# Earlier bias transfers, a new order of the first stage, and four products of batch 1 on GpSimd

## The reference

```python
x = x + L0(x)   # masked softmax over blocks of 128 tokens, pooled @ x, divided by the count
x = x + L1(x)   # zX*lap_x + zY*lap_y + zR*y*(1-y); lap_x along the 512 channels, lap_y along tokens
x = x + L2(x)   # z = relu(x@Wd + bd); y = x + z@Wu + bu; layernorm(y)*g + b
x = x + L3(x)   # below
# L3: ctx = causal_ema(x); wg = sigmoid([x, ctx] @ Wg + bg); h1 = gelu(x @ Wn1 + bn1)
#     mod = 0.5 + sigmoid(h1 @ Wn2 + bn2); traces_d = causal_ema(x*wg*mod_d)
#     gate = sigmoid(blend(traces) @ Wtemp + btemp); soma = gelu(x @ Wsoma + bsoma)
#     out = layernorm((soma*gate) @ Wout) * gamma + beta
```

## Time and profile before

| | us |
|---|---|
| median of 3 runs | 744.46 (743.62 to 744.91) |
| profiled execution | 746.6 |
| its span | 744.8 |
| PE busy | 676.6 (91%) |
| DVE busy | 539.8 (72%) |
| ACT busy | 351.0 (47%) |
| POOL busy | 175.4 (24%) |

### The profile page before, as it was taken

One profiled execution on the slowest core, in us unless ns is written; L12 is line 12 of the kernel. 1 busy time (PEld: TensorE's weight loads), 2 busy tenths in 40 slices (PEclk: granted clock), 3 DMA queues, 4 the chain that ended last, 5 costly groups with the idle time before them and its releaser, 6 DMA issues.

```text
span 744.8 us, 7950 instructions
## 1 busy us (share of the span) xinstructions
PE 676.6 (91%) x2808; PEld 495.2 (66%) x2808; DVE 539.8 (72%) x736; ACT 351.0 (47%) x710; POOL 175.4 (24%) x220
## 2 busy tenths in 40 slices
PE   4979976465699999999999999999999999999996
PEld 1544443234486877787777868786877787787874
DVE  3558984458799669667875976697669768875964
ACT  1142475254445733563465347344733563465144
POOL 5004337425344110220032111202210220031001
PEclk9989998867899999999999999999999999999999
DMA  7991698668944474147326434551474050314001
GB/s 211 296 389 65 179 298 200 130 191 288 295 107 79 57 147 80 57 76 150 58 70 131 82 57 113 116 95 20 110 153 74 0 114 2 56 19 96 0 2 56
DMA packets 52470, 87.87 MB, mean 118 GB/s; under 512 B 8256, under 2 KB 10304, under 8 KB 52430
## 3 DMA queue, kind: packets, MB, share of 16 engines
q0 software_dynamic: 16896, 33.56, 27.9%
q1 hardware_dynamic: 32046, 53.79, 21.0%
q10 hardware_dynamic: 3488, 0.01, 0.3%
HBM read 64.27 MB, written 23.09 MB: 117 GB/s over the span
## 4 chain that ended last, share of the span: by engine, by line
PE 77%; DVE 12%; DMA 3%; issue 3%; ACT 2%; POOL 1%; SPq 1%; POOLq 0%; DVEq 0%; ACTq 0%
PE bank L1051 20%; PE bank L1053 19%; PE bank L1052 19%; PE bank L1107 4%; PE bank L1091 3%; PE bank L1047 2%; PE bank L1154 2%; DMA xr<-rows_scratch 2%; PE bank L1116 2%; PE bank L952 2%; PE bank L1081 2%; DVE xts L1411 2%; DMA xts<-in_xT 1%; DVE xb L1398 1%; DVE xts L1404 1%
## 5 line engine op out<-in xcount | busy, mean ns | idle before, releaser
L1506 DVE TENSOR_TENSOR_SCAN tr<-alpha,carry,tr 128x512 f32<-128x512 f32 x48 | 58.9, 1268 | 0.0
L1500 DVE SCALAR_TENSOR_TENSOR tr<-wgb,blend_w,mod 128x512 f32<-128x512 f32 x64 | 46.0, 750 | 10.7 <-ACT mod L765 9.9
L546 POOL TENSOR_TENSOR xts<-xb 128x2040 f32<-128x2040 f32 x8 | 31.5, 3937 | 93.5 <-DVE xb L1398 59.1
L1051 PE MATMUL bank<-xh,wg_l 128*128 128x512 f32 x128 | 53.0, 414 | 0.0
L1051 PE MATMUL bank<-th,wg_l 128*128 128x512 f32 x128 | 52.0, 406 | 0.0
L1052 PE MATMUL bank<-xl,wg_h 128*128 128x512 f32 x128 | 50.6, 395 | 0.0
L1053 PE MATMUL bank<-xh,wg_h 128*128 128x512 f32 x128 | 50.4, 393 | 0.0
L1053 PE MATMUL bank<-th,wg_h 128*128 128x512 f32 x128 | 50.1, 391 | 0.0
L1052 PE MATMUL bank<-tl,wg_h 128*128 128x512 f32 x128 | 49.9, 390 | 0.0
L1398 DVE SCALAR_TENSOR_TENSOR xb<-bank,rnorm,xb 128x512 f32<-128x512 f32 x32 | 23.7, 748 | 31.5 <-PE bank L1048 31.5
L780 ACT ACTIVATE carry<-tr 128x2 f32<-128x2 f32 x32 | 6.5, 203 | 74.8 <-DVE tr L1506 74.8
(11 more groups left out here) (246 smaller groups left out, 1963.0 us busy)
## 6 DMA issues: line engine op xcount, KB each, us to landing
x2b<-beside_scratch POOLq DMA_DIRECT2D x12, 1024.0 KB, 10.3
xr<-rows_scratch POOLq DMA_DIRECT2D x10, 1024.0 KB, 9.6
xb<-in_x SPq DMA_DIRECT2D x8, 1024.0 KB, 14.6
beside_scratch<-xb SPq DMA_DIRECT2D x8, 1024.0 KB, 6.2
result<-xr SPq DMA_DIRECT2D x7, 1024.0 KB, 10.5
local_scratch<-xts SPq DMA_DIRECT2D x6, 1024.0 KB, 9.3
x2b<-local_scratch SPq DMA_DIRECT2D x6, 1024.0 KB, 5.5
x2b<-rows_scratch POOLq DMA_DIRECT2D x6, 1024.0 KB, 9.4
```

The source lines that it names most:

```text
L546: po.tensor_tensor(side[:, :, 1:E - 1], xg[:, :, 0:E - 2], xg[:, :, 2:E], ALU.add)\
L1051: pe.matmul(acc, wl, xh_, start=start, stop=False)
L1500: ve.scalar_tensor_tensor(t[:, d], w, blend_w[:, d, k:k + 1], mod[:, d], ALU.mult, ALU.mult).then_inc(tr_in, 1)
L1506: ve.tensor_tensor_scan(t[:, d], alpha[:, 1 + d:2 + d].broadcast_to([P, GN]), t[:, d], 0.0 if first else carry[:, k, 1 + d:2 + d], ALU.mul ...
```

## The change

Two kinds of edit. First, bias and order: the bias row of L2 is added to x2 as the first of its three adding transfers (for blocks 0 and 1 when their stencil is done, for the others when the block is back from DRAM, one or two turns ahead); so the transposed x2 holds the bias, and `x2_evict` takes it off again with `-up_cols`. `y_sum` has no wait for it any more. The orders of all five engines in stage 1 change, the parameter work of DVE moves to the front in smaller pieces, `load_adapter(1)` and others move in SP's list, the tiles xh, xl, x2b1, hb1 and wn2_rep are laid out otherwise, and the wait for `local_done` before the copies of wn2 is gone. Second, `by_local(4)` to `by_local(7)` go from DVE to POOL, each ahead of the `channels` of its block.

```diff
+x2b1 = sb2("x2b1", [P, GT, E])
+xh = sb2("xh", [P, KE, GN], F32R)
+xl = sb2("xl", [P, KE, GN], F32R)
-sb2("between", [P, 1280])
-xh = sb2("xh", [P, KE, GN], F32R)
-xl = sb2("xl", [P, KE, GN], F32R)
-x2b1 = sb2("x2b1", [P, GT, E])
...
-mix_v = sem("mix_v")
+mix_v = [sem(f"mix_v{b}") for b in range(B)]
...
     for i, t in enumerate((row_bu, row_s)):
         sp.dma_start(rows_dram[b:b + 1, i], t[2 * Q * b:2 * Q * b + 1]).then_inc(rows_out, 16)
 store_beside(0)
-store_beside(1)
 sp.wait_ge(rows_out, 16 * 2 * B)
 sp.dma_start(gamma_row[:], row(gamma, P)).then_inc(rows2_in, 16)
 for b in range(B):
     pid = sp.value_load(ids[0:1, b:b + 1], min_val=0, max_val=7)
     sp.dma_start(ln_g_row[:, b], ln_g[bass.ds(pid, 1), :].broadcast_to([P, E]))\
       .then_inc(rows2_in, 16)
+store_beside(1)
 sp.wait_ge(hid_mm, 2 * NG)
 sp.dma_start(wg_st[:, 0:KE], chunks(wg)[:, 0:KE]).then_inc(w_in[0], 16)
 store_beside(2)
+store_local(2)
 sp.dma_start(wg_st[:, KE:], chunks(wg)[:, KE:]).then_inc(w_in[1], 16)
-store_local(2)
 store_beside(3)
+load_x2(2)
 store_local(3)
-sp.wait_ge(blog_set, B)
-sp.wait_ge(score_use, B * NG)
-load_adapter(sp, 1, sp.value_load(ids[0:1, 1:2], min_val=0, max_val=7))
 store_beside(4)
 store_local(4)
-load_x2(2)
 store_beside(5)
 store_local(5)
 beside_landed(sp, 1, 0)
...
+sp.wait_ge(blog_set, B)
+sp.wait_ge(score_use, B * NG)
+load_adapter(sp, 1, sp.value_load(ids[0:1, 1:2], min_val=0, max_val=7))
 out_v = out.rearrange("b (u c p) e -> p (b u) c e", p=P, c=GT)
...
     po.tensor_scalar(side[:, :, E - 1:E], xg[:, :, E - 2:E - 1], 2.0, None, ALU.mult)\
       .then_inc(chan, 1)
-def add_before(q):
-    b, j = q // NG, q % NG
+def by_local(n):
+    s = local_of(n).rearrange("p g e -> p (g e)")
+    po.wait_ge(mix_u, n + 1)
+    po.tensor_tensor(s, s, x1_of(n).rearrange("p g e -> p (g e)"), ALU.mult).then_inc(mix_v[1], 1)
+
+def add_up_bias(q):
+    if q == 0:
+        po.wait_ge(rows_out, 16 * 2 * B)
     if q < 2:
         po.wait_ge(local_done, q + 1)
     else:
         po.wait_ge(x2_in, 16 * (q - 1))
+    add_row(q, 0, x2_of(q), row_add)
+
+def add_before(q):
+    b, j = q // NG, q % NG
+    po.wait_ge(row_add, 16 * (q + 1))
     beside_landed(po, b, j - 1)
     beside_landed(po, b, j)
     po.dma_start(x2_of(q), beside_rows(b, j, -1), accum_op=ALU.add).then_inc(before_add, 16)
...
-def add_up_bias(q):
-    if q == 0:
-        po.wait_ge(rows_out, 16 * 2 * B)
-    po.wait_ge(x2T_mm, KE * q + KE)
-    add_row(q, 0, x2_of(q), row_add)
-    add_row(q, 1, xr[:, q % 2], shift_add)
+    add_row(q, 1, xr[:, q % 2], shift_add[q % 2])
...
+add_up_bias(0)
 channels(1)
 add_before(0)
+add_up_bias(1)
+add_after(0)
 channels(2)
-add_after(0)
 weight_low(0, wn1_h[:], wn1_l[:], wn1_st[:])
+add_before(1)
 channels(3)
-add_before(1)
-add_up_bias(0)
+add_after(1)
 weight_low(1, wg_h[:, 0:KE], wg_l[:, 0:KE], wg_st[:, 0:KE])
-add_after(1)
-weight_low(2, wg_h[:, KE:], wg_l[:, KE:], wg_st[:, KE:])
+by_local(4)
 channels(4)
 for c in range(GT):
     rstd(ln_ss, ss_a, EPSILON, rs_a, c, ln_p, ln_rs, c)
+weight_low(2, wg_h[:, KE:], wg_l[:, KE:], wg_st[:, KE:])
+by_local(5)
 channels(5)
 add_shift(0)
+add_up_bias(2)
+by_local(6)
 channels(6)
+by_local(7)
 channels(7)
 weight2_low(1, ws_h[:], ws_l[:], ws_st[:])
 for g in range(GROUPS):
...
             weight2_low(2, wo_h[:], wo_l[:], wo_st[:])
         add_after(g + 2)
+    if g == 0:
+        weight2_low(3, wt_h[:], wt_l[:], wt_st[:])
     if g < LAST:
-        add_up_bias(g + 1)
-        if g == 0:
-            weight2_low(3, wt_h[:], wt_l[:], wt_st[:])
         for c in range(GT):
             rstd(ln_ss, ss_a, EPSILON, rs_a, GT * (g + 1) + c, ln_p, ln_rs, c)
         add_shift(g + 1)
+    if g + 3 < GROUPS:
+        add_up_bias(g + 3)
     for c in range(GT):
...
-        act.activation(wide[:, k], bank[X2T(q)[k]][:], ACT.Copy).then_inc(x2T_ev, 1)
+        act.activation(wide[:, k], bank[X2T(q)[k]][:], ACT.Identity,
+                       bias=up_cols[:, q // NG, k:k + 1]).then_inc(x2T_ev, 1)
...
+act.wait_ge(params_in, N_PARAMS)
+act.activation(alpha[:], taus[:], ACT.Exp).then_inc(setup_a, 1)
 tanh(0, 2)
 weights(0, 0)
 tanh(0, 3)
 weights(0, 1)
+act.wait_ge(params_set, 3)
+act.activation(blend_w[:], blend_t[:, 0:2], ACT.Exp).then_inc(setup_a, 1)
 weights(0, 2)
 weights(0, 3)
 act.wait_ge(pool_const, 7)
...
     probT_evict(0, j)
 mix_local(0)
 tanh(1, 0)
-act.wait_ge(params_in, N_PARAMS)
-act.activation(alpha[:], taus[:], ACT.Exp).then_inc(setup_a, 1)
+scale_beside(0)
 tanh(1, 1)
-act.wait_ge(params_set, 3)
-act.activation(blend_w[:], blend_t[:, 0:2], ACT.Exp).then_inc(setup_a, 1)
-scale_beside(0)
-mix_local(1)
 weights(1, 0)
 tanh(1, 2)
 weights(1, 1)
+mix_local(1)
 tanh(1, 3)
+weights(1, 2)
 scale_beside(1)
-weights(1, 2)
 weights(1, 3)
-mix_local(2)
 block_exps(1)
 prob_exps(1)
 sums_raw(1)
-wg_hi(2, wn1_h[:], wn1_st[:])
-scale_beside(2)
 sums_hi(1)
+mix_local(2)
 for j in range(NG):
     bw_evict(1, j)
 for j in range(NG):
     probT_evict(1, j)
+wg_hi(2, wn1_h[:], wn1_st[:])
+scale_beside(2)
 mix_local(3)
+act.wait_ge(params_set, S_PARAMS)
+x2_evict(0)
+scale_beside(3)
 wg_hi(0, wg_h[:, 0:KE], wg_st[:, 0:KE])
-scale_beside(3)
-x2_evict(0)
-wg_hi(1, wg_h[:, KE:], wg_st[:, KE:])
 act.wait_ge(cols_in, 16 * 3 * B)
 relu(0)
 act.wait_ge(rows2_in, 16 * (1 + B))
...
 mix_local(5)
-act.wait_ge(params_set, S_PARAMS)
 beside_landed(act, 0, 3)
 x3_evict(0)
 scale_beside(5)
 mix_local(6)
+scale_beside(6)
 mix_local(7)
-scale_beside(6)
 weight_hi(0, ws_h[:], ws_st[:])
 scale_beside(7)
 for g in range(GROUPS):
...
-for c in range(6):
+for c in range(4):
     pooled(0, c)
 hidden(1, 0)
-pooled(0, 6)
-pooled(0, 7)
+pooled(0, 4)
+pooled(0, 5)
 hidden(1, 1)
 scores(1, 0)
-pooled(0, 8)
+pooled(0, 6)
 hidden(1, 2)
 scores(1, 1)
-pooled(0, 9)
+pooled(0, 7)
 hidden(1, 3)
 scores(1, 2)
-pooled(0, 10)
+pooled(0, 8)
 scores(1, 3)
-pooled(0, 11)
 block_sums(1, 0)
 block_sums(1, 1)
-pooled(0, 12)
+pooled(0, 9)
+pooled(0, 10)
 block_sums(1, 2)
+pooled(0, 11)
 block_sums(1, 3)
 weight_sums(1)
-pooled(0, 13)
+pooled(0, 12)
 replicate(1)
-pooled(0, 14)
-pooled(0, 15)
+for c in range(13, NT):
+    pooled(0, c)
 for j in range(NG):
     block_transposes(1, j)
 for j in range(NG):
...
-    ve.tensor_tensor(s, s, flat(x1_of(n)), ALU.mult).then_inc(mix_v, 1)
+    ve.tensor_tensor(s, s, flat(x1_of(n)), ALU.mult).then_inc(mix_v[0], 1)
-    ve.wait_ge(mix_v, n + 1)
+    ve.wait_ge(mix_v[b], n % NG + 1)
...
+def params_alpha():
-    ve.wait_ge(cols_in, 16 * 3 * B)
-    param(ve.tensor_tensor(shift_cols[:], shift_cols[:], up_cols[:], ALU.subtract))
-def params_b():
+def params_blend():
-                                          ALU.mult, ALU.mult))
+                                          ALU.mult, ALU.mult), False)
+def params_cols():
+    ve.wait_ge(cols_in, 16 * 3 * B)
+    param(ve.tensor_tensor(shift_cols[:], shift_cols[:], up_cols[:], ALU.subtract))
+    param(ve.tensor_scalar(up_cols[:], up_cols[:], -1.0, None, ALU.mult), False)
-    if c == 0:
-        ve.wait_ge(row_add, 16 * (q + 1))
...
-        ve.wait_ge(shift_add, 16 * (g + 1))
+        ve.wait_ge(shift_add[g % 2], 16 * (g // 2 + 1))
...
-for j in range(NG):
-    read_scores(0, j)
+read_scores(0, 0)
+params_raw()
+read_scores(0, 1)
+params_alpha()
+read_scores(0, 2)
+read_scores(0, 3)
 softmax_in(0)
 normalise_out(0)
 normalise(0)
+params_blend()
 sums_low(0)
+params_cols()
+rows()
 for c in range(6):
     x1(0, c)
-rows()
-x1(0, 6)
-x1(0, 7)
 by_local(0)
 stencil(0)
-params_a()
+x1(0, 6)
 read_scores(1, 0)
+read_scores(1, 1)
+x1(0, 7)
+by_local(1)
+read_scores(1, 2)
 x1(0, 8)
-params_b()
-read_scores(1, 1)
+stencil(1)
+read_scores(1, 3)
+softmax_in(1)
 x1(0, 9)
-by_local(1)
-stencil(1)
-read_scores(1, 2)
 x1(0, 10)
 x1(0, 11)
-read_scores(1, 3)
-softmax_in(1)
+normalise_out(1)
 x1(0, 12)
+by_local(2)
 x1(0, 13)
-by_local(2)
-normalise_out(1)
+sums_low(1)
 x1(0, 14)
+x1(0, 15)
 stencil(2)
 normalise(1)
-sums_low(1)
-x1(0, 15)
 x1(1, 0)
 x1(1, 1)
 by_local(3)
...
 x1(1, 2)
 x1(1, 3)
 x1(1, 4)
-x1(1, 5)
 for c in range(GT):
     y_sum(0, c)
+x1(1, 5)
 x1(1, 6)
+for c in range(GT):
+    ln_weigh(0, c)
 x1(1, 7)
-ln_weigh(0, 0)
-ln_weigh(0, 1)
-x1(1, 8)
-ln_weigh(0, 2)
-ln_weigh(0, 3)
-x1(1, 9)
 for c in range(GT):
     ln_apply(0, c)
-by_local(4)
 stencil(4)
+x1(1, 8)
+x1(1, 9)
 x1(1, 10)
 x1(1, 11)
-by_local(5)
-stencil(5)
+x3_lo(0)
 x1(1, 12)
 x1(1, 13)
-x3_lo(0)
+stencil(5)
 x1(1, 14)
 x1(1, 15)
-by_local(6)
 stencil(6)
-by_local(7)
 stencil(7)
-ve.wait_ge(local_done, GROUPS)
 for d in range(2):
```

More of the change, by code:

```diff
@@ L29 @@
 N_PARAMS = 16 * 10
-S_MASKS, S_ROWS, S_PARAMS = 29, 2, 13
+S_MASKS, S_ROWS, S_PARAMS = 29, 2, 14
 POOL_N = 26
@@ L165, in build_program @@
         row_add = sem("row_add")
-        shift_add = sem("shift_add")
+        shift_add = [sem(f"shift_add{i}") for i in range(2)]
         down_mm = sem("down_mm")
@@ L716, in scale_beside @@
                         b = n // NG
-                        act.wait_ge(mix_v, n + 1)
```

(5 more changed lines are left out.)

## The result

| | before | after |
|---|---|---|
| median of 17 runs each, us | 744.56 (743.2 to 747.5) | 747.15 (745.87 to 753.08) |
| ratio, with its 95% interval | | 1.004 (1.0024 to 1.0057) |
| profiled execution / its span | 746.6 / 744.8 | 748.79 / 747.0 |
| first MOD product | 194.25 | 197.41 |
| span behind it | 550.5 | 549.6 |

The changed kernel is 0.4% slower, where 738.5 was forecast. The stretches of the changed kernel, in the columns of the earlier trace rows, say where: stage 2 is what it was, so the loss lies ahead of MOD. POOL has 30.6 of the 45 us before 195.

What follows compares the result with a forecast made beforehand. PE bounds stage 2, a constant 550.5 us behind the first MOD product, so that start sets the time: 161 + 27.4 = 188.4 against 194.25, 5.9 earlier, from median 744.46 to 738.5; range 731 to 746.5.

Steps and rivals of the forecast that it cites:

- The order part: Stage 1, new orders and early bias: x1(0, 15) ends about 105 instead of 108.7, first y_sum 124.7 instead of 135.75.
- S5: End of stencil(5) in stage 1: forecast at 161 us, against 169.0 before.
- The four `rstd`: POOL, block 0, behind channels(4) ending at 135.2: done by 138.9, where they ended at 143.0 before.
- the contest behind them: POOL's weight_low(2), ready at 139.1, against the last ln_apply at 139.0; if POOL wins, everything behind is 4.5 us later.
- From S5 to MOD: Way from the end of stencil(5) to the first MOD product: 27.4 us, 2.1 more than before, MOD at 188.4.
- I take 10.4: Store of block 5, with two adding transfers just ahead of it: 10.4 us, where 8.1 was measured before.
- Product 7 3.6: by_local(7) on POOL, between mix_local(7) and channels(7): 3.6 us, taken from the undisturbed channels row of 3.58.
- Its own sign of being wrong: End of stage 1: the forecast is wrong if mix_local(7) waits more than 12 us after S5.
- Rival 2: Store of block 5 comes late among other transfers, 19.1 us counted: MOD at 197.0, time 747.3; chance 0.11.
- Rival 1: GpSimd sets the pace: each product takes 4.5 us or loses a turn, 3.6 added over four, 742.1; chance 0.16.
- Rival 3: End of stage 1: stencil gets ahead of weight2_low(1), or S5 comes at 157; 4.5 us less, 734; chance 0.13.
- Rival 4: Order changes don't reach the end of stage 1: stencil(5) still ends at 169, 2.1 us added, 746.6; chance 0.06.

Runs made afterwards that it cites:

- e1: Changed kernel with add_up_bias(2) issued behind weight2_low(1) instead of ahead of by_local(6) on POOL; 742.05 us, ratio 0.9972.
- e10: e1 with add_shift(0) also moved behind weight2_low(1); 742.38 us, ratio 0.9965 against the kernel before.
- e9: e1 with the products of blocks 6 and 7 on DVE, those of 4 and 5 on POOL; 736.06 us, ratio 0.9902.
- e5: e3 with ACT's weight_hi(0) moved behind the first gelu; 737.67 us, ratio 0.9914 against the kernel before.
- e12: e5 with POOL's weight2_low(2) ahead of add_before and weight2_low(3) ahead of add_after in its first turn; 736.26 us, ratio 0.9888.
- e8: e1 with POOL's channels(7) ahead of by_local(7), all four products on POOL; 740.01 us, ratio 0.9935.
- e3: Changed kernel with both edits: add_up_bias(2) behind weight2_low(1) and the four products back on DVE; 735.71 us, ratio 0.9873.
- e2: Changed kernel with the four products of batch 1 back on DVE, each ahead of its stencil; 736.12 us, ratio 0.9881.
- e4: Kernel before with only by_local(4) to by_local(7) moved to POOL, each ahead of its channels; 745.61 us, ratio 1.0011.
- e6: Changed kernel with another form of POOL product for each of blocks 4 to 7; blocks 4, 6, 7 took 4.48, 3.96, 3.54 us start to start.
- e11: e5 with add_shift(0) also issued late, behind weight2_low(1); 743.63 us, ratio 0.9984 against the kernel before.

## Why the prediction was wrong

**What held.** The way of reading did: stage 2 is a constant, and the first MOD product sets the time in every kernel that leaves the weight parts alone. The order part held up to the first `y_sum`: eviction 109.1 (forecast 111.5), `y_sum` 122.3 (124.7). PE was ready at 175.4 (175). POOL's queue was right until `channels(4)`, 126.5 and 134.97 (126 and 135.2), the second by luck: the product took 0.9 more than forecast, and what followed up to `rstd` 0.8 less.

**S5: 163.1 instead of 161.** Two errors that nearly cancel. The four `rstd` took 6.9 us (134.97 to 141.9) and not 3.7, and the contest behind them was lost, the end of the range that the prediction named: `stencil(4)` ended at 153.4 instead of 146.3. The way from there to S5 was 9.7 instead of 14.7, because product 5 went ahead of `stencil(4)` instead of behind it: it is part of the lateness of `stencil(4)` and not of what follows. That S5 came out within 2.1 is luck in part.

**The step that failed: "From S5 to MOD", 27.4.** It was 34.3, and these 6.9 decide the sign. Two of its terms were off. "I take 10.4" for the store: it was 16.6, so `mix_local(7)` started 16.65 behind S5 and not 10.5, 6.15 of the 6.9. "Product 7 3.6": it was 4.5, by the other end that the prediction held. The rest was right within 0.3 each. The 10.4 was 8.1 with a little added for two adding transfers; e1 and e10 price them: 5.5 us of landing with none, 11.3 with one, 16.6 with both issued 4 to 5 us ahead. The 8.1 was no measure of one such transfer: before, the shift went out 8.3 us ahead of the store, after 4.8. The prediction had a row of 19.0 in the earlier trace rows and gave it to a rival. Its own sign of being wrong, `mix_local(7)` over 12 us behind S5, came true with 16.65.

**The rivals.** Rival 2 was right in place: the landing of 16.6 passed the 16.3 from which it counted a loss. It said MOD at 197.0 and 747.3, measured 197.41 and 747.15; that this is so close is luck, as it had 19.1 for the landing, 2.5 too many, against an S5 2.1 too early and a product 0.9 too short. It got 0.11. Rival 1 was right in the size of the product (4.5) and wrong in its sum over four: products 4 and 5 cost nothing on balance (e9), product 7 costs 2.7, about 4.0 are left for product 6. Rival 3's lost turn has no worth that the runs can tell (e5, e12). Rival 4 fell: S5 moved from 169 to 163.1.

**What the sum did not ask.** It set product 7 and `channels(7)` behind each other, 3.6 and 4.0, and so they ran, 4.5 and 3.9: this is not the step that failed. But it never set that order against one in which POOL does `channels(7)` beside `mix_local(7)`. From the start of `mix_local(7)` to MOD that makes 14.9 us with the product behind it on POOL (e8) and 13.6 with the product on DVE (e3), against 17.6. Taken apart, the change is a good one and a bad one: order and early bias alone 0.9881 (e2), the products alone 1.0011 (e4), both 1.004.

The Trainium skill, GPSIMD Engine Reference, section "Elementwise — side-by-side cycle accounting", gives 4497 ns for a float32 `tensor_tensor` of 2048 columns (an addition there). The changed kernel's 4.50 agrees, and e6's addition shows the same row as the product; the 3.58 that spoke against it in the earlier trace rows is of the other kind, both inputs in one tile and the output elsewhere.

## What to carry to other kernels

Work moved to a less busy engine is paid for by its place in that engine's queue: ask which of its instructions could run while the moved one is still waiting for its input, and put them ahead, or leave the work where it is. A transfer has to be priced with those that were issued a few microseconds before it; a landing measured without such company is only its lower bound, and if the sum decides its sign by that number, the worse row of the trace belongs in the forecast. After a change of two parts try each part alone: here the two together hid a gain of 1.2%.

## What the runs showed of the hardware

- A 1 MB store from SP's queue landed in 5.5, 11.3 or 16.6 us with none, one or two adding transfers of 1 MB issued in the 5 us before it (e10, e1, after); in these three SP's own store of x1, also 1 MB, stands 2.6 us ahead. e8, e9 and e4, with one each, have 11.4, 11.0 and 10.9, e6 with two again 16.6. With two that went out 8.6 and 9.5 us ahead it takes 12.0 (e2), here with SP's store of x1 only 0.4 us ahead.
- With one adding transfer 10 us ahead it takes 7.6 (e3), and with none at all ahead of it 7.8 (e11): that transfer costs nothing any more. In both SP's store of x1 stands only 0.4 us ahead, which goes with the 7.6 and 7.8 against the 5.5 of e10; no run moves it alone. From e11:

```profile
L385 SPq DMA_DIRECT2D local_scratch<-xts x1: 488/488/488, 162.5 to 162.5; - x1
...
DMA to landing us min/median/max: 7.8/7.8/7.8
```

- POOL takes 4.5 us for 2048 columns of two float32 tiles, written over one of them, and 3.96 (2048 columns) or 3.54 (2040) when both inputs lie in one tile and the output in another (e6).
- A DVE operation that finds POOL at work can wait for its end even as a plain copy with one input. In e2 two copies of 128 columns take 4.65 us instead of 0.35:

```profile
179.52 4.65 DVE L1632 COPY wn_rep<-wn_col 128x128 f32<-128x128 f32 x2
```

```profile
178.18 5.77 POOL L584 TENSOR_TENSOR ws_l<-ws_l_f,ws_h 128x2048 fp32r<-128x2048 f32 x1 [4.89 <-ACT ws_h L831]
```

The POOL row began at 178.18 and had itself waited for `stencil(7)`, so the two copies stood until it ended at 183.9. The Trainium skill, SBUF — State Buffer, section "Who interferes with whom", says that a copy too can contend with GpSimd, where its operands allow a mode that takes both of VectorE's ports. The 4.65 agree; which mode the copy ran in, no run shows.
